# A three-layer sweep over an 8192 x 8192 matrix: part of the upper triangle by seven products in place of eight

## The chip, the cores and the metric

The kernel runs on one core of one Trainium2 chip. Times are device microseconds of that core from the start to the end of an execution. The trace is one profiled execution, taken by the hardware profiler: for each engine the instructions with start and duration, and the inferred releaser of every wait. TensorE (PE) does matrix products, with its weight loads (PEld) shown apart; VectorE (DVE), ScalarE (ACT) and GpSimd (POOL) work on tiles in SBUF; SyncE (SP) only issues DMA transfers. Each engine takes its instructions in order; they wait for each other by semaphores.

## What is computed

Four graph layers over the same adjacency matrix `adj`, 8192 x 8192 in float32, and node features `x`, 8192 x 64:

```python
def reference(x, adj, L0_gnn_u, L1_gnn_W, L1_gnn_b, L2_gnn_W, L3_gnn_W):
    h = relu(layernorm(x));  x = x + adj @ (h * (u >= 0.1) / 0.9)                            # layer 0
    h = relu(layernorm(x));  z = concat([h, (adj @ h + h) / deg]) @ W1 + b1                  # layer 1
    out = relu(z);           x = x + out / max(norm(out), 1e-12)
    h = relu(layernorm(x));  x = x + (dinv[:, None] * (adj + I) * dinv[None, :]) @ h @ W2    # layer 2
    h = relu(layernorm(x));  x = x + concat([h, adj @ h / (rowsum(adj) + 1)]) @ W3.T         # layer 3
    return x
```

Each layer needs `adj` times the states of the layer before it, row by row of the result, and row b's new states need all of row b.

## The kernel before, in words

`adj` is cut into 16 x 16 units of 512 x 512 (1 MB each, 128 partitions by 2048 numbers: four source tiles of 512 columns). Unit (b, g) holds what source block g gives to row b. A matmul has one source tile's states as weights (64 columns for one layer, 128 for two layers at once) and 512 columns of the unit as the moving operand; the result adds up in a PSUM bank of 128 x 512, whose lower 64 partitions (half 0) and upper 64 (half 1) are addressed apart. Each unit has four matmuls per layer; the trace shows each as two records.

The order is a sweep by phases, so that one loaded unit serves two layers where it can. Phase 1 goes down the rows for layer 0, with layer 1 in the part below the diagonal. Phase 2 goes up through the upper triangle for layer 1 (the units above the diagonal) and layer 2. Phase 3 goes down for layers 2 and 3, phase 4 does the rest of layer 3. `loads_in_order` writes out the load order for SP; the units go through a ring of 12 slots, a slot is reloaded when its unit has been let go (`unit_freed`), and diagonal units have two tiles of their own (`diag`).

The stretch that is changed is phase 2 after its head (rows 14 to 11 are the head, done by `head_first` and `head_second`): the loop over b from 10 down to 0 in the TensorE block. For each row b it takes the sources g from 15 down to b+1, 110 units in all, with `both_at_once` (line 563): four matmuls of 128 weight columns, layer 1's states (`h[1]`) in the lower half of the array and layer 2's (`h[0]`) in the upper, into one bank. Row b's source g needs the layer-2 states of row g, which the end of row g made (`await_unit` waits for them).

- After its first unit a row does `finish(1, b + 1)` (line 584): four matmuls of the gathered sums of the row before by the layer's weights, into Z. After its third it does `turn_own(1, b)` (line 627): two transposes of the row's own scaled states into HT, which ScalarE's `copy_hT` (line 398) copies to the upper half of y.
- VectorE does per row: `gather_1` (line 946: layer 1's sum from the bank to y), `end_layer_1` (lines 913 to 962, then the layer norm, lines 877 to 921: the new states of layer 2, with two square roots asked of ScalarE, `norm_root`, line 375), and `scale_own` (line 1031).
- ScalarE copies the layer-2 sum from the bank (`copy_part`, line 391) once Z is done.
- GpSimd makes constants at the start and clears one tile (line 355) in the head; in the loop it has nothing.

After the loop comes phase 3 with `head_first(3, ...)`, for which VectorE adds one to four diagonals (`add_one_again`, line 1006) after ScalarE has kept copies of them in `row_sum` (`keep_diag`). In phase 1 VectorE sums the units for the degrees (`sum_unit`, line 979, one unit-sized addition each).

## Time and profile before

| | |
|---|---|
| median of 3 runs | 1935.79 us (1935.2 to 1936.11) |
| span of the profiled execution | 1935.0 us |
| TensorE busy | 1892.8 us, 98% |
| VectorE busy | 855.0 us, 44% |
| ScalarE, GpSimd busy | 115.2 us, 3.3 us |
| DMA | 670.30 MB, 346 GB/s over the span |
| granted TensorE clock | 9 (nine tenths or more) in all 40 slices |

A page of the profile gives busy time by engine, the span in 40 slices, the chain of waits that ended last, and groups of instructions by line, operation and tile. The views used below are the page, the windows (busy time of each engine in a stretch), the timeline (instructions in order of time), the chain of waits in order of time, and the groups. Times on the chain and the timeline are us from the start of the span. Matmuls overlap in the records: one of 512 columns is recorded with about 0.59 us while the next starts 0.43 after it, so what counts is the step from one to the next.

### The profile page before, as it was taken

What the parts mean: (1) busy time and instruction counts of PE and PEld (TensorE: products, weight loads), DVE (VectorE), ACT (ScalarE), POOL (GpSimd) and SP (SyncE); (2) the same over time, 40 slices, a digit from 0 to 9 for tenths busy, and PEclk for the clock granted to TensorE, in tenths of its full rate; (3) what the DMA queues carried; (4) which work ended last, traced back from release to release, by engine and by line L of the source; (5) the groups of instructions that cost most, each with busy time, mean ns of one, the idle gap of its engine ahead of it and who ended that gap; (6) DMA issues with size and microseconds to landing.
All of it is one profiled execution on the core that took longest, in us unless ns stands there. A gap on an engine that the chain in (4) does not pass through costs nothing.

```text
span 1935.0 us, 17870 instructions
## 1 busy us (share of the span) xinstructions
PE 1892.8 (98%) x7216; PEld 740.1 (38%) x7216; DVE 855.0 (44%) x1023; ACT 115.2 (6%) x293; POOL 3.3 (0%) x18
## 2 busy tenths in 40 slices
PE   5899999999999999999999999999999999999998
PEld 1233333333333333444444444344444444344343
DVE  8677999998877763622112111321211110110322
ACT  0000000000000001100000000111100000000000
POOL 0000000000000000000000000000000000000000
PEclk9999999999999999999999999999999999999999
DMA  9999999999888885598888887497999989999998
GB/s 382 422 421 420 421 421 421 421 421 377 341 322 318 305 300 197 204 362 288 298 298 288 300 294 274 169 400 287 399 383 364 344 309 423 373 357 416 356 422 338
DMA packets 95168, 670.30 MB, mean 346 GB/s; under 512 B 11120, under 2 KB 13168, under 8 KB 14192
## 3 DMA queue, kind: packets, MB, share of 16 engines
q1 hardware_dynamic: 92160, 666.94, 87.9%
q10 hardware_dynamic: 2928, 2.23, 0.3%
q8 instruction: 59, 0.97, 0.2%
q14 instruction: 21, 0.17, 0.0%
HBM read 667.03 MB, written 2.10 MB: 346 GB/s over the span
## 4 chain that ended last, share of the span: by engine, by line
PE 86%; DVE 6%; DMA 6%; issue 1%; ACT 0%; SPq 0%; DVEq 0%
PE acc L534 45%; PE acc L563 36%; DMA ring<-stream_in 6%; PE Z L584 3%; DVE row_sum L979 1%; PE HT L627 1%; PE DEG L595 1%; DVE states L921 0%; DVE squares L880 0%; DVE centred L878 0%; PE DEG L604 0%; DVE inverse L881 0%; DVE mean L877 0%; DVE z_sb L913 0%; DVE x L962 0%
## 5 line engine op out<-in xcount | busy, mean ns | idle before, releaser
L534 PE MATMUL acc<-ring,states 128*64 128x512 f32 x4160 | 926.3, 596 | 34.2 <-DMA ring<-stream_in 26.5
L563 PE MATMUL acc<-ring,states 128*128 128x512 f32 x1792 | 778.8, 593 | 0.0
L534 PEld LDWEIGHTS acc<-ring,states 128*64 128x64 f32 x4160 | 296.6, 137 | 615.1 <-issue 586.2
L563 PEld LDWEIGHTS acc<-ring,states 128*128 128x128 f32 x1792 | 336.7, 190 | 414.5 <-issue 414.5
L979 DVE TENSOR_TENSOR row_sum<-row_sum,ring 128x2048 f32<-128x2048 f32 x187 | 428.5, 2292 | 9.1 <-DMA ring<-stream_in 3.9
L913 DVE TENSOR_TENSOR z_sb<-Z,deg_rsqrt 128x256 f32<-128x256 f32 x16 | 6.8, 425 | 336.8 <-PE Z L584 336.8
L946 DVE TENSOR_TENSOR y<-acc,y 64x512 f32<-64x512 f32 x16 | 11.1, 692 | 282.3 <-PE acc L563 274.9
L534 PE MATMUL acc<-diag,states 128*64 128x512 f32 x448 | 103.8, 595 | 1.1 <-DMA diag<-stream_in 1.1
L391 ACT COPY y<-acc 64x512 f32<-64x512 f32 x45 | 26.1, 580 | 1005.0 <-PE acc L534 730.6
L584 PEld LDWEIGHTS Z<-below,y 128*128 128x128 f32 x512 | 62.9, 191 | 50.6 <-issue 16.6
L1040 DVE TENSOR_TENSOR y<-acc,y 64x512 f32<-64x512 f32 x36 | 24.6, 683 | 111.3 <-PE acc L534 111.0
L584 PE MATMUL Z<-below,y 128*128 128x64 f32 x512 | 69.6, 279 | 2.2 <-DVE y L1041 2.2
L534 PEld LDWEIGHTS acc<-diag,states 128*64 128x64 f32 x448 | 32.5, 137 | 67.5 <-issue 64.7
L1006 DVE TENSOR_TENSOR diag<-diag,ident 128x384 f32<-128x384 f32 x12 | 6.7, 559 | 106.8 <-ACT row_sum L410 106.8
L979 DVE TENSOR_TENSOR row_sum<-ring 128x2048 f32<-128x2048 f32 x16 | 36.7, 2292 | 31.6 <-DMA ring<-stream_in 30.7
L929 DVE TENSOR_TENSOR x<-Z,x 128x256 f32<-128x256 f32 x16 | 6.8, 425 | 71.9 <-PE Z L584 71.6
L985 DVE TENSOR_TENSOR row_sum<-row_sum,diag 128x2048 f32<-128x2048 f32 x16 | 36.7, 2293 | 1.7 <-DMA diag<-stream_in 1.1
L375 ACT ACTIVATE rooted<-to_root 128x4 f32<-128x4 f32 (+1 forms) x68 | 14.0, 206 | 331.3 <-DVE to_root L867 303.2
L398 ACT COPY y<-HT 64x256 f32<-64x256 f32 x64 | 23.4, 365 | 153.9 <-PE HT L627 153.5
L877 DVE TENSOR_REDUCE mean<-x 128x4 f32<-128x256 f32 (+1 forms) x52 | 25.0, 481 | 7.7 <-DMA y<-u_in 6.0
L1041 DVE TENSOR_TENSOR y<-acc,y 64x512 f32<-64x512 f32 x36 | 24.9, 693 | 1.2
L913 DVE TENSOR_TENSOR z_sb<-Z,deg_clipped_inverse 128x256 f32<-128x256 f32 x16 | 6.8, 424 | 38.5 <-PE Z L584 38.4
(78 smaller groups left out, 363.2 us busy)
## 6 DMA issues: line engine op xcount, KB each, us to landing
ring<-stream_in SPq DMA_DIRECT2D x604, 1024.0 KB, 9.0
diag<-stream_in SPq DMA_DIRECT2D x28, 1024.0 KB, 11.5
x<-x_in SPq DMA_DIRECT2D x4, 512.0 KB, 6.9
y<-u_in SPq DMA_DIRECT2D x4, 512.0 KB, 8.7
x_out<-x ACTq DMA_DIRECT2D x16, 128.0 KB, 7.1
below<-w_in ACTq DMA_DIRECT2D x6, 16.0 KB, 5.8
bias<-b_in ACTq DMA_DIRECT2D x1, 32.0 KB, 9.8
```

The costliest lines, as they stand in the source:

```text
L391: nc.scalar.copy(own_y(b, 1 if layer == 2 else 0), half_of(bank, half)).then_inc(part_copied, 1)
L398: done = nc.scalar.copy(by_parity[:, parity], turned)
L534: return nc.tensor.matmul(half_of(bank, half), h[layer % 2][:, J], moving, start=start, stop=stop)
L563: done = nc.tensor.matmul(acc[bank][:, :], states[:, J * 2 * F:(J + 1) * 2 * F], source_tile(slot(key), k), start=first and k == 0, stop=l ...
L584: mm_z = nc.tensor.matmul(Z[:, t * F:(t + 1) * F], own_y(b)[:, t * P:(t + 1) * P], below[:, layer, :], start=True, stop=True)
L595: nc.tensor.matmul(DEG[k * QUARTER:(k + 1) * QUARTER, :], pick(key[1]), source_tile(slot(key), k), start=key == (1, 0, PE_SUMS[0][0]), sto ...
L627: mm_t = nc.tensor.transpose(HT[:, columns], scaled[n % 2][:, columns], ident[:, :])
L877: chain(nc.vector.tensor_reduce(m, by_tile(xs), X, ALU.add))
L979: nc.vector.tensor_tensor(row_sum[:, :], before, slot(key)[:, :], ALU.add).then_inc(unit_summed, 1 if count > 1 else 2)
L985: chain(nc.vector.tensor_tensor(row_sum[:, :], row_sum[:, :], diag_slot(1, b)[:, :], ALU.add))
L1040: chain(nc.vector.tensor_tensor(own_y(r, 0), half_of(bank, 0), own_y(r, 0), ALU.add))
L1041: nc.vector.tensor_tensor(own_y(r, 0), half_of(bank, 1), own_y(r, 0), ALU.add).then_inc(group_folded, 1)
```

## The change

Rows 10 to 1 of the loop are taken as five pairs (hi, lo), and sources above them as pairs (s1, s2). For such a group of four units (a **four**: A11 = (hi, s1), A12 = (hi, s2), A21 = (lo, s1), A22 = (lo, s2)) and the states B of the two sources in the two layers, the eight products of 2 x 2 blocks are replaced by seven (Strassen's scheme in Winograd's form). There are 2, 3, 4, 4 and 4 fours in the pairs, 17 in all.

- VectorE makes four new units per four from those in the ring, one unit-sized operation each: the sum A21 + A22 (into `row_sum` or `row_totals`) and A11 - A21 in `first_forms`, and the two that overwrite A11 and A12 in `last_forms`. The latter wait until TensorE has used the plain ones (`first_taken`, `second_taken`).
- GpSimd makes four combinations of states per source pair once (128 x 256 each), into the `diag` tiles, which are free until phase 3.
- TensorE does the products with weights of 64 columns, in slots of two products at a time, one in each half: an even four (`four_even`) in four slots, P2 with P1, P5 with P4, P7 with P6, and P3 with P1 of the next four ("P1 again", in a bank of its own); an odd four (`four_odd`) in three, P2 with P4, P5 with P6, P7 with P3. The products add up in banks over the fours of a pair (`GATHERS`).
- The unit (lo, hi) next to the diagonal is used for layer 1 in its own pair and loaded again for layer 2 ("again", "behind") in the next: `near_diagonal` does both as one slot, and in the first and the last pair one of the two is alone. The sources that make no pair are done by `plain_both`, one slot for each unit. The loads rise from 110 to 115 units.
- VectorE puts the sums together (`combine`, `combine_low`, `add_behind`) in place of `gather_1` and ScalarE's `copy_part`, with 64 x 512 additions.
- Row 0 is no longer the last row: two of its units stand at the start of every pair (`cover`) and the other five after the last.
- `finish` for both rows of a pair and the two transposes of the next pair stand between and behind these units; then TensorE waits for `pair_taken`. SP's diagonal loads of phase 3 wait for the last pair's end.

```diff
+PAIRS = [(10, 9), (8, 7), (6, 5), (4, 3), (2, 1)]
+SOURCE_PAIRS = [(15, 14), (13, 12), (11, 10), (9, 8)]
+FOURS = [[sp for sp in SOURCE_PAIRS if sp[1] > hi] for hi, lo in PAIRS]
+FOURS_BEFORE = [sum(len(fours) for fours in FOURS[:p]) for p in range(len(PAIRS) + 1)]
+PLAIN = [list(range(min(s for sp in FOURS[p] for s in sp) - 1, PAIRS[p][0], -1)) for p in range(len(PAIRS))]
+COVER = [[15, 14], [13, 12], [11, 10], [9, 8], [7, 6], [5, 4, 3, 2, 1]]
...
-BANK_UP = {13: 0, 12: 2, 11: 4, 14: 3, 10: 1}
-for b in range(9, -1, -1):
-    BANK_UP[b] = BANK_UP[b + 5]
+BANK_UP = {13: 0, 12: 2, 11: 4, 14: 3, 0: 1}
+GATHERS = {"P2": (0, 0), "P1": (0, 1), "P5": (2, 0), "P4": (2, 1), "P7": (4, 0), "P6": (4, 1),
+           "P1 again": (3, 0), "P3": (3, 1), "plain": (5, 0), "behind": (5, 0)}
...
-    for b in range(LAST - 1 - HEAD, -1, -1):
-        out += [(2, b, g) for g in range(LAST, b, -1)]
+    for p, (hi, lo) in enumerate(PAIRS):
+        out += [(2, 0, g) for g in COVER[p]]
+        for i, (s1, s2) in enumerate(FOURS[p]):
+            if i == len(FOURS[p]) - 1:
+                out += [("again", *PAIRS[p - 1][::-1])] if p else []
+                out += [(2, lo, hi)]
+            out += [(2, lo, s1), (2, lo, s2), (2, hi, s1), (2, hi, s2)]
+        out += [(2, b, g) for g in PLAIN[p] for b in (hi, lo)]
+    out += [(2, 0, g) for g in COVER[-1][:-1]] + [("again", *PAIRS[-1][::-1]), (2, 0, COVER[-1][-1])]
...
+            gp.wait_ge(*diag_let_go(1, LAST))
+            for n, (s1, s2) in enumerate(SOURCE_PAIRS):
+                gp.wait_ge(*state(2, s2))
+                if n > 0:
+                    gp.wait_ge(states_formed, n)
+                (b11, b12), (b21, b22) = [[of_row_states(layer, b) for layer in (1, 2)] for b in (s1, s2)]
+                t1, t2, t3, t4 = [formed((s1, s2), t) for t in (1, 2, 3, 4)]
+                nc.gpsimd.tensor_tensor(t1, b12, b11, ALU.subtract).then_inc(gp_step, 1)
+                nc.gpsimd.tensor_tensor(t3, b22, b12, ALU.subtract).then_inc(gp_step, 1)
+                gp.wait_ge(gp_step, 7 + 3 * n + 2)
+                nc.gpsimd.tensor_tensor(t2, b22, t1, ALU.subtract).then_inc(gp_step, 1)
+                gp.wait_ge(gp_step, 7 + 3 * n + 3)
+                nc.gpsimd.tensor_tensor(t4, b21, t2, ALU.subtract).then_inc(states_formed, 1)
...
+            for p in range(len(PAIRS)):
+                act.wait_ge(*pair_done(p))
+                if p > 0:
+                    act.wait_ge(pair_taken, 3 * p)
+                nc.scalar.copy(pair_sum(0), product("P1")).then_inc(p1_copied, 1)
+                for b in PAIRS[p + 1] if p < len(PAIRS) - 1 else [0]:
+                    copy_hT(1, b)
+                for b in PAIRS[p]:
                     norm_root()
                     norm_root()
-                copy_hT(1, b)
-                if b == 0:
-                    for r in ADDED[:HEAD]:
-                        keep_diag(r)
+            act.wait_ge(*fours_taken(FOURS_BEFORE[-1] - 1))
...
+            def four_even(p, i):
+                (hi, lo), (s1, s2) = PAIRS[p], FOURS[p][i]
+                n, last = FOURS_BEFORE[p] + i, i == len(FOURS[p]) - 1
+                a11, a12, a21, a22 = [(2, b, g) for b in (hi, lo) for g in (s1, s2)]
+                await_unit(a12, 1)
+                await_unit(a11, 1)
+                for k in range(TPR):
+                    two = nc.tensor.matmul(product("P2"), h[1][:, s2 * TPR + k], source_tile(slot(a12), k),
+                                           start=i == 0 and k == 0, stop=False)
+                    one = nc.tensor.matmul(product("P1"), h[1][:, s1 * TPR + k], source_tile(slot(a11), k),
+                                           start=i == 0 and k == 0, stop=i >= len(FOURS[p]) - 2 and k == TPR - 1)
+                two.then_inc(second_taken, 1)
+                one.then_inc(first_taken, 1)
+                pe.wait_ge(states_formed, SOURCE_PAIRS.index((s1, s2)) + 1)
+                pe.wait_ge(unit_formed, 4 * n + 1)
+                await_unit(a22, 2)
+                for k in range(TPR):
+                    five = nc.tensor.matmul(product("P5"), formed((s1, s2), 1)[:, k], source_tile(first_sum[n % 2], k),
+                                            start=i == 0 and k == 0, stop=last and k == TPR - 1)
+                    four = nc.tensor.matmul(product("P4"), formed((s1, s2), 4)[:, k], source_tile(slot(a22), k),
+                                            start=i == 0 and k == 0, stop=False)
+                five.then_inc(sum_taken, 1)
+                four.then_inc(unit_freed, 1)
+                pe.wait_ge(unit_formed, 4 * n + 3)
+                for k in range(TPR):
+                    seven = nc.tensor.matmul(product("P7"), formed((s1, s2), 3)[:, k], source_tile(slot(a21), k),
+                                             start=i == 0 and k == 0, stop=last and k == TPR - 1)
+                    nc.tensor.matmul(product("P6"), formed((s1, s2), 2)[:, k], source_tile(slot(a11), k),
+                                     start=i == 0 and k == 0, stop=last and k == TPR - 1)
+                seven.then_inc(unit_freed, 1)
+                pe.wait_ge(unit_formed, 4 * n + 4)
+                if not last:
+                    t1, t2 = FOURS[p][i + 1]
+                    await_unit((2, hi, t1), 1)
+                for k in range(TPR):
+                    if not last:
+                        one = nc.tensor.matmul(product("P1 again"), h[1][:, t1 * TPR + k],
+                                               source_tile(slot((2, hi, t1)), k), start=i == 0 and k == 0,
+                                               stop=i >= len(FOURS[p]) - 3 and k == TPR - 1)
+                    three = nc.tensor.matmul(product("P3"), h[0][:, s2 * TPR + k], source_tile(slot(a12), k),
+                                             start=i == 0 and k == 0, stop=False)
+                if not last:
+                    one.then_inc(first_taken, 1)
+                three.then_inc(unit_freed, 2)
+            def four_odd(p, i):
...
+                pe.wait_ge(states_formed, SOURCE_PAIRS.index((s1, s2)) + 1)
+                await_unit(a12, 1)
+                await_unit(a22, 2)
...
+                two.then_inc(second_taken, 1)
+                pe.wait_ge(unit_formed, 4 * n + 3)
...
+                five.then_inc(sum_taken, 1)
+                six.then_inc(unit_freed, 1)
+                pe.wait_ge(unit_formed, 4 * n + 4)
...
+                seven.then_inc(unit_freed, 1)
+                three.then_inc(unit_freed, 2)
...
+            def behind_last():
+                hi, lo = PAIRS[-1]
+                await_unit(("again", lo, hi), 2)
+                pe.wait_ge(pair_taken, 3 * len(PAIRS))
...
+            for p, (hi, lo) in enumerate(PAIRS):
+                cover(COVER[p][0])
+                if p > 0:
+                    finish(1, PAIRS[p - 1][0])
+                cover(COVER[p][1])
+                if p > 0:
+                    finish(1, PAIRS[p - 1][1])
+                turn_own(1, hi)
+                turn_own(1, lo)
+                if p == 0:
+                    pe.wait_ge(*gathered(1, 11))
+                    pe.wait_ge(part_copied, PARTS.index((2, 11)) + 1)
+                else:
+                    pe.wait_ge(pair_taken, 3 * p)
+                for i in range(len(FOURS[p])):
+                    if i == len(FOURS[p]) - 1:
+                        near_diagonal(p)
+                    if i % 2 == 0:
+                        four_even(p, i)
+                    else:
+                        four_odd(p, i)
+                for g in PLAIN[p]:
+                    plain_both(p, g)
+            cover(COVER[-1][0])
+            finish(1, PAIRS[-1][0])
+            cover(COVER[-1][1])
+            finish(1, PAIRS[-1][1])
+            turn_own(1, 0)
+            cover(COVER[-1][2])
+            cover(COVER[-1][3])
+            behind_last()
+            cover(COVER[-1][4])
...
+            def first_forms(p, i):
+                (hi, lo), (s1, s2) = PAIRS[p], FOURS[p][i]
+                n = FOURS_BEFORE[p] + i
+                a11, a21, a22 = (2, hi, s1), (2, lo, s1), (2, lo, s2)
+                dve.wait_ge(*loaded(a21))
+                dve.wait_ge(*loaded(a22))
+                if n >= 2:
+                    dve.wait_ge(*fours_taken(n - 2))
+                nc.vector.tensor_tensor(first_sum[n % 2][:, :], slot(a21)[:, :], slot(a22)[:, :],
+                                        ALU.add).then_inc(unit_formed, 1)
+                dve.wait_ge(unit_formed, 4 * n + 1)
+                dve.wait_ge(*loaded(a11))
+                nc.vector.tensor_tensor(slot(a21)[:, :], slot(a11)[:, :], slot(a21)[:, :],
+                                        ALU.subtract).then_inc(unit_formed, 1)
+                dve.wait_ge(unit_formed, 4 * n + 2)
+            def last_forms(p, i):
+                (hi, lo), (s1, s2) = PAIRS[p], FOURS[p][i]
+                n = FOURS_BEFORE[p] + i
+                a11, a12 = (2, hi, s1), (2, hi, s2)
+                dve.wait_ge(first_taken, n + 1)
+                nc.vector.tensor_tensor(slot(a11)[:, :], first_sum[n % 2][:, :], slot(a11)[:, :],
+                                        ALU.subtract).then_inc(unit_formed, 1)
+                dve.wait_ge(unit_formed, 4 * n + 3)
+                dve.wait_ge(second_taken, n + 1)
+                nc.vector.tensor_tensor(slot(a12)[:, :], slot(a12)[:, :], slot(a11)[:, :],
+                                        ALU.subtract).then_inc(unit_formed, 1)
+                dve.wait_ge(unit_formed, 4 * n + 4)
+            def combine(p):
+                hi, lo = PAIRS[p]
+                y_hi, y_lo, some, more = own_y(hi, 0), own_y(lo, 0), pair_sum(0), pair_sum(1)
+                dve.wait_ge(*pair_done(p))
+                chain(nc.vector.tensor_tensor(y_hi, product("P2"), y_hi, ALU.add))
+                dve.wait_ge(p1_copied, p + 1)
+                chain(nc.vector.tensor_tensor(some, product("P1 again"), some, ALU.add))
+                nc.vector.tensor_tensor(y_hi, some, y_hi, ALU.add).then_inc(sums_ready, 1)
+                dve.wait_ge(*gathered(1, hi))
+                chain(nc.vector.tensor_tensor(some, product("P6"), some, ALU.add))
+                chain(nc.vector.tensor_tensor(more, product("P7"), some, ALU.add))
+                chain(nc.vector.tensor_tensor(y_lo, more, y_lo, ALU.add))
+                nc.vector.tensor_tensor(y_lo, product("P4"), y_lo, ALU.add).then_inc(sums_ready, 1)
+                dve.wait_ge(*gathered(1, lo))
+                chain(nc.vector.tensor_tensor(pair_sum(0, 1), product("P5"), some, ALU.add))
+                nc.vector.tensor_tensor(pair_sum(1, 1), product("P5"), more, ALU.add).then_inc(pair_taken, 1)
+                dve.wait_ge(pair_taken, 3 * p + 1)
+                begin_layer_1(hi)
+                nc.vector.tensor_tensor(own_y(hi, 1), product("P3"), pair_sum(0, 1), ALU.add).then_inc(pair_taken, 1)
+                dve.wait_ge(pair_taken, 3 * p + 2)
+            def combine_low(p):
+                lo = PAIRS[p][1]
+                dve.wait_ge(z_done, rank(1, lo) + 1)
+                nc.vector.tensor_tensor(own_y(lo, 1), product("plain"), pair_sum(1, 1),
+                                        ALU.add).then_inc(pair_taken, 1)
+                dve.wait_ge(pair_taken, 3 * p + 3)
+            def add_behind(p):
+                hi, lo = PAIRS[p]
+                dve.wait_ge(*freed(("again", lo, hi)))
+                nc.vector.tensor_tensor(own_y(lo, 1), product("behind"), own_y(lo, 1),
+                                        ALU.add).then_inc(behind_added, 1)
+                dve.wait_ge(behind_added, p + 1)
...
+            for p, (hi, lo) in enumerate(PAIRS):
+                if p > 0:
+                    combine(p - 1)
+                first_forms(p, 0)
+                if p > 0:
+                    combine_low(p - 1)
+                last_forms(p, 0)
+                first_forms(p, 1)
+                last_forms(p, 1)
+                if p > 0:
+                    end_layer_1(PAIRS[p - 1][0], begun=True)
+                for i in range(2, len(FOURS[p])):
+                    first_forms(p, i)
+                    if i == len(FOURS[p]) - 1:
+                        add_behind(p - 1)
+                    last_forms(p, i)
+                if p > 0:
+                    end_layer_1(PAIRS[p - 1][1])
+                for b in PAIRS[p + 1] if p < len(PAIRS) - 1 else [0]:
+                    scale_own(1, b)
+            combine(len(PAIRS) - 1)
+            end_layer_1(PAIRS[-1][0], begun=True)
+            combine_low(len(PAIRS) - 1)
+            end_layer_1(PAIRS[-1][1])
+            add_behind(len(PAIRS) - 1)
+            gather_1(0)
```

`cover(g)` is `both_at_once` on unit (0, g). In `near_diagonal` (which waits for layer 2's states of the pair before it, `await_unit("again", 2)`), `plain_both` and `behind_last` each k does one matmul per half as above; `plain_both` waits for both layers' states of its source and, in the lower row's first unit, for `behind_added`.

## Rows read from the trace of the kernel before

**Rows 1.** The page: busy time, VectorE by slice, GB/s by slice, and the loop's matmuls.

```profile
PE 1892.8 (98%) x7216; PEld 740.1 (38%) x7216; DVE 855.0 (44%) x1023; ACT 115.2 (6%) x293; POOL 3.3 (0%) x18
...
DVE  8677999998877763622112111321211110110322
...
GB/s 382 422 421 420 421 421 421 421 421 377 341 322 318 305 300 197 204 362 288 298 298 288 300 294 274 169 400 287 399 383 364 344 309 423 373 357 416 356 422 338
...
L563 PE MATMUL acc<-ring,states 128*128 128x512 f32 x1792 | 778.8, 593 | 0.0
```

**Rows 2.** Windows: length, then busy PE, PEld, DVE, ACT, POOL; clock, DMA share, GB/s.

```profile
807.39:1200.06 392.67, 391.33 (x983) 177.13 (x982) 70.41 (x192) 21.74 (x63) 0.00 (x0) 1.00 0.86 308
440.00:640.00 200.00, 200.00 (x950) 68.20 (x948) 157.03 (x104) 7.20 (x15) 0.00 (x0) 1.00 0.89 337
```

**Rows 3.** Timeline at the loop's end: start, duration, engine, line, tiles, idle time before.

```profile
1200.26 0.69 DVE L946 TENSOR_TENSOR y<-acc,y 64x512 f32<-64x512 f32 x1 [41.73 <-PE acc L563]
```

**Rows 4.** Chain of waits in row 3 of the loop: start, duration, what.

```profile
1020.72 34.34 PE acc L563 x80
1055.05 0.85 PE Z L584 x8
```

**Rows 5.** The same chain, at half-width stretches of phases 1 and 3.

```profile
703.75 34.48 PE acc L534 x160
...
1226.91 7.02 PE acc L534 x32
...
1243.70 3.63 PE acc L563 x8
...
1257.85 5.29 PE acc L534 x16
...
1285.57 5.30 PE acc L534 x24
1290.87 1.03 PE Z L584 x8
```

**Rows 6.** Timeline, end of row 4 in the loop (rows between left out).

```profile
1008.99 0.69 DVE L946 TENSOR_TENSOR y<-acc,y 64x512 f32<-64x512 f32 x1 [28.00 <-PE acc L563]
1012.22 1.00 PE L584 MATMUL Z<-below,y 128*128 128x64 f32 x8
...
1013.26 0.42 DVE L913 TENSOR_TENSOR z_sb<-Z,deg_clipped_inverse 128x256 f32<-128x256 f32 x1 [3.58 <-PE Z L584]
1013.72 0.42 DVE L950 TENSOR_TENSOR z_sb<-z_sb,bias 128x256 f32<-128x256 f32 x1
...
1019.34 0.42 DVE L921 SCALAR_TENSOR_TENSOR states<-centred,inverse 128x256 f32<-128x256 f32 x1
...
1020.28 0.44 PE L627 MATMUL HT<-ident,scaled 128*128 128x128 f32 x2
...
1020.75 0.74 ACT L398 COPY y<-HT 64x256 f32<-64x256 f32 x2 [1.85 <-PE HT L627]
```

**Rows 7.** Groups by shape, whole span: busy us, mean ns of one, idle before.

```profile
L979 DVE TENSOR_TENSOR row_sum<-row_sum,ring 128x2048 f32<-128x2048 f32 x187 | 428.5, 2292 | 9.1 <-DMA ring<-stream_in 3.9
...
L979 DVE TENSOR_TENSOR row_sum<-ring 128x2048 f32<-128x2048 f32 x16 | 36.7, 2292 | 31.6 <-DMA ring<-stream_in 30.7
...
L946 DVE TENSOR_TENSOR y<-acc,y 64x512 f32<-64x512 f32 x16 | 11.1, 692 | 282.3 <-PE acc L563 274.9 <-ACT y L452 7.3
```

**Rows 8.** Timeline, phase 3: TensorE starts again after a wait for VectorE.

```profile
1223.25 0.42 DVE L921 SCALAR_TENSOR_TENSOR states<-centred,inverse 128x256 f32<-128x256 f32 x1
...
1223.82 2.06 PE L534 MATMUL acc<-ring,states 128*64 128x512 f32 x8 [1.17 <-DVE states L921]
```

**Rows 9.** The ring's loads in a stretch of the loop, issue to landing.

```profile
DMA to landing us min/median/max: 4.7/4.8/7.2
```

**Rows 10.** GpSimd's groups of instructions, whole span.

```profile
L337 POOL TENSOR_SCALAR_AFFINE_SELECT ident<-ident 128x128 f32<-128x128 f32 x1 | 0.3, 292 | 0.1
...
L355 POOL MEMSET y<- 64x512 f32 x1 | 0.5, 519 | 772.0 <-PE Z L584 772.0
```

149 lines of the change are left out of this document (121 added, 28 removed).

## Prediction

> **What bounds the kernel now.** I read the page first [rows 1]: TensorE is busy 98% of the span at full clock (the granted clock is 1.00 in every stretch I asked for), VectorE 44%, and in the slices of the upper-triangle loop (18 to 24 of 40) VectorE has one to two tenths. Then the windows [rows 2]: the loop, from its first matmul at 807.39 to 1200.06, where the last unit has issued (0.20 before VectorE reads it at 1200.26 [rows 3]), lasts 392.67 us; TensorE is busy 391.3 of them, VectorE 70.4, GpSimd 0, and the DMA moves 308 GB/s, where 421 to 423 are reached in other slices [rows 1]. The loop's matmuls (L563) have no idle time ahead of them at all [rows 1]. So in the one stage that the change touches the end is set by TensorE's column work: a change gains what it takes from TensorE, as long as VectorE, which gets new work, stays ahead.
>
> The chain of waits prices one unit [rows 4]: 10 whole units (128-wide weights, eight records each) take 34.34 us, so a **slot is 3.43 us**. A finish (Z) between whole units adds 0.85, a transpose pair 0.44 [rows 6]. 110 units make 377.4 us; finishes, transposes and their small waits are the other 15.3. Half-width matmuls run two at a time: 160 records, ten slots of 16, take 34.48 us, 32 take 7.02 with the switch to Z behind them [rows 5]. So a pair of half matmuls with different moving data costs the same slot. Between whole and half there is a surcharge: 3.63 for the last whole unit ahead of a transpose (0.20), 5.30 for one and a half slots ahead of Z (0.15), and 1.03 for a Z followed by halves (0.18) [rows 5]. A half without a partner costs its whole slot: a diagonal unit of row 4, which has none, and half a slot make 16 records in 5.29 us, where 24 records take 5.30 [rows 5].
>
> **The change on TensorE.** The 17 groups of four units are 68 units. By products they take 7 slots for two fours, 4 for an even one: 7+11+14+14+14 = 60 slots over the five pairs of rows. The five units next to the diagonal become six slots (one layer each, now paired across rows, the first and the last without a partner). The 11 sources left over stay at one slot per unit, 22; row 0 stays at 15. Sum 60+6+22+15 = 103 slots in place of 110: **7 x 3.43 = 24.0 us less**. That the two halves now carry different products into different banks costs nothing: the head steps (32 records in 7.02 [rows 5]) already do this. Against it: transposes come back to back, and the second waits until ScalarE has copied the first (0.74 for the copy [rows 6]), 1.75 for two in place of two times 0.44 and a small wait: over the loop +2.5. Whole-to-half switches, where no wait hides them: 5 x 0.15 at the pairs' ends and about 0.8 more: +1.6. TensorE alone would thus come out at -19.9, and VectorE decides what is left of it.
>
> **VectorE's prices.** A unit-sized operation (128x2048, two tiles of the ring) takes 2.292 us [rows 7], with the gap to the next 2.33. The 64x512 addition from PSUM takes 0.69, with its gap 0.73 [rows 7]; I take that for the additions in SBUF too. The scaled z is 0.46. The rest of the end of a row is 1013.72 to 1019.76 = 6.04 us, 6.5 with the z [rows 6]. A VectorE operation starts 0.20 us after the slot it waits for has issued (1012.22 less one slot is 1008.79, and it starts at 1008.99 [rows 6]); TensorE restarts 0.15 after the VectorE operation it waits for ends (1223.67 to 1223.82 [rows 8]). VectorE gets four unit-sized operations per four, 17 x 9.3 = 158 us, and 60 additions of 0.73 (eleven a pair and the one of the unit behind), 44, less ten gathers, 7; with the 70 it has that is some 265 of 398 us. So in total it fits; phase 1 shows TensorE undisturbed beside a VectorE that is busy 157 of 200 us [rows 2]. What matters is the order, since both engines take their work in order. I placed it on two time lines, E being the moment at which TensorE has issued a pair's last unit.
>
> (a) Entry of each pair after the first. TensorE: switch 0.15, cover 3.43, finish 0.86, cover 3.43, finish 0.86, two transposes 1.75: E+10.5. Then it waits for pair_taken, which combine_low raises. VectorE: E+0.20, ten additions and the z in combine (7.76), **both first_forms (4.66) which stand ahead of combine_low**, combine_low 0.73: E+13.35, so TensorE starts at 13.5. Wait **3.0, four times: 12.1**.
> (b) Two fours, T being their start: the even one (four slots) ends at T+13.7, the odd one (three) at T+24.0. VectorE starts last_forms 0.20 after the first slot, at 3.6, and has the two at 6.0 and 8.3; TensorE asks for them at 6.9 and 10.3. The next first_forms follow at 10.6 and 12.95, ahead of their use at 17.2. The odd last_forms wait for P1 (13.7) and P2 (17.15): 16.25 and 19.7, used at 17.2 and 20.6. No wait, with 0.7 to 2 us of margin.
> (c) Third four. end_layer_1 of the upper row stands ahead of its first_forms: VectorE is through at 19.7+6.04 = 25.7, then 28.05, 30.4, and 32.7 for the first of last_forms. TensorE needs the first sum at T+27.4 (gets it at 28.2) and the next form at 31.6 (gets it at 32.9). **0.8 + 1.2 = 2.0, in three pairs: 6.0.** In the pair (8, 7) the slot beside the diagonal comes first and needs row 10's new states: 25.9 against 24.0, 1.9, and hides the rest.
> (d) The plain source after the last four needs the states of the lower row before it: in (8, 7) 1.2, in (6, 5) 55.6+0.15 against 53.4 = 2.3. (The 55.6 is the fourth four's last form, at 49.1, and 6.5; the 53.4 is seven slots after the 28.2 of (c), with its 1.2.) In the last two pairs other sources come first: none.
> (e) Last pair's end: row 0's source 2 waits for row 2's states, for whose root ScalarE comes late, as it has the transpose of row 0 ahead of it: 2.0.
> Waits together 12.1+6.0+1.9+3.5+2.0 = **25.5 us**. Net: -24.0 + 2.5 + 1.6 + 25.5 = +5.6. With stretches added instead the loop is 398.1 against 392.7, **+5.5 us**: the first pair 43.1, then 64.6, 76.2 (as 13.5 of entry, 53.4 of fours, 2.3 of wait and 6.9 for one plain source), 87.6, 101.3, and 25.4 for the end of row 0. With gaps of 0.02 to 0.03 more per operation and 0.05 per wait it is +9; with the small ones all less, +3.4.
>
> Other edits at nothing: ScalarE's P1 copy is 0.58 beside VectorE's first addition; its ten copies of parts go; the five extra loads (115 units in 398 us, one per 3.46, while one lands in 2.5 us at 421 GB/s) lie inside the margin, and every four has its four units issued over 10 us before VectorE wants them, against 4.8 us median from issue to landing [rows 9]. SP's diagonal load that now waits for the last pair comes behind ring loads that are freed later anyhow. row_sum is kept for the diagonals only after the last four; ScalarE's four copies end before row 0's gather, as before. What follows the loop is as before and moves along.
>
> GpSimd's 16 subtractions (128x256) have no row of their kind; the nearest are 0.29 (128x128) and 0.52 (64x512 memset) [rows 10]. I take 0.3 to 0.8 each, the smaller and the sum of the two. The four in a row behind row 10's new states leave 3 us or more to spare. Whether they slow VectorE is not in the trace: nothing to, at worst, their whole time.
> The Trainium skill speaks against this part (GPSIMD Engine Reference, Specifications and Key points): GpSimd shares its SBUF interfaces with VectorE, with contention for instructions with two SBUF inputs, which all forms are; section 3.1 gives about 2.6 cycles per element at 1.2 GHz, an estimate of 0.6 to 0.7 us for one of these. No run here shows it yet.
>
> **Rivals.**
> Forecast, 65%: as placed, +5.5, from +3 to +9. About a third of it (+3.9 or less) would be within 0.2%.
> The entry is covered, 15%: faster. The mechanism is (a): if VectorE gets through its list at a pair's entry while TensorE is still in the two row-0 units, the four waits go; from 1.4 us less each the change is no loss, with all gone it is 5.5 - 12.1 = -6.6 us (1929), and with (c) to (e) gone too -19.9 (1916). For it: VectorE has over 130 us free in the loop, and some of its additions are from SBUF alone, for which I have no row. Against it: only two of the ten are, and the unit-sized operations, 4.66 of the 13.2 us, have 187 rows at 2.292.
> GpSimd holds VectorE up, 15%: the four operations follow directly on end_layer_1 of rows 10 and 8, just when VectorE does first_forms of the third four. If their 1.2 to 3.2 us are added to VectorE there, waits (c) and (d) grow by as much in two pairs, up to +4: 1943 to 1946. It decides from 1 us of hold-up per four operations. This is the Trainium skill's rule named above made into a time.
> Loads late, 5%: a four needs all its units at once. If the 7.2 us that is the longest landing [rows 9] became the rule at bursts of four, and each third four waited 2 us more for it, 6 us in all: 1947.
> That products don't save slots: excluded by [rows 5].
>
> **How the numbers follow.** The profiled execution has a span of 1935.0, the median of the runs is 1935.79, 0.8 above. 1935.0 + 5.5 + 0.8 = **1941.3 us**. For 8 in 10: down into the forecast's lower side and a little of the second case, 1934; up to GpSimd's case and a late load, 1948. A change under 0.2% (3.9 us) can hardly be told from none. Slower: 43 of the 65, and 15 and 5: 63%. Within: 22%. Faster 15%.
>
> **What would show it.** TensorE wait on y written by combine_low about 3 us, four times, and on ring units written by VectorE 0.8 and 1.2 us in the rows (6, 5), (4, 3), (2, 1); one wait each on states of rows 10, 9, 7 and 2. The loop some 398 us long, matmul busy time 20 us or more lower. It is wrong if these waits are absent (then the time is near 1916 to 1929), if half pairs with different products take over 3.5 us per slot, or if forms take clearly over 2.3 us.

## The result, and the profile after

| | before | after |
|---|---|---|
| median, lowest to highest | 1935.65 us (1935.20 to 1936.11, 4 runs) | 1951.56 us (1950.07 to 1953.65, 4 runs) |
| ratio, with 95% interval | | 1.0084 (1.0071 to 1.0098) |
| span of the profiled execution | 1935.0 us | 1951.0 us |
| TensorE busy | 1892.8 us | 1882.9 us |
| mean granted TensorE clock of the span | 1.00 | 0.993 |
| the loop, first matmul to its end | 392.8 us | 410.05 us |

The change makes the kernel 16 us slower. I had forecast 5.5 us slower, 1941.3, and a range up to 1948: the sign is right, the time lies outside the range. The page of after, with busy times and VectorE's and the clock's slices, answers to [rows 1]:

```profile
PE 1882.9 (97%) x7840; PEld 700.0 (36%) x7840; DVE 1047.9 (54%) x1141; ACT 112.0 (6%) x288; POOL 27.5 (1%) x34
...
DVE  8778999998888762857767564421211110110332
...
PEclk9999999999999999999999999999999999999999
```

TensorE works 9.9 us less, and the kernel is longer: the rest is standing still. VectorE has four to seven tenths in the slices of the loop, where it had one or two. The row of the clock shows nothing, since a slice is 49 us long; it takes short windows to see it, as below.

The loop alone, as a window (columns: length, busy time with count of TensorE, its weight loads, VectorE, ScalarE and GpSimd, granted clock, DMA share, GB/s), answers to [rows 2]:

```profile
806.95:1217.00 410.05, 382.05 (x1607) 138.63 (x1606) 262.00 (x310) 18.53 (x58) 17.89 (x8) 0.97 0.77 308
```

It is 17.3 us longer than before. The rest of the span gives 1.3 back (0.4 ahead of the loop, 0.9 behind), which makes the 16.0. The granted clock is 0.97, where it was 1.00. TensorE's waits in the loop (engine, line and what it waited for, then us in total, times, longest):

```profile
PE acc L783 <- DVE y L1251: 11.0, 4, 2.8
PE HT L718 <- ACT y L480: 4.6, 5, 0.9
PE acc L801 <- DVE ring L1217: 3.7, 3, 1.8
PE acc L877 <- DVE states L1167: 3.0, 2, 2.2
PE acc L651 <- DVE states L1167: 2.0, 1, 2.0
PE acc L793 <- issue: 1.8, 3, 0.6
PE DEG L861 <- DVE states L1167: 1.8, 1, 1.8
```

The first is (a), the wait for combine_low at the entries of four pairs. L801 and L793 are (c), L861 the slot beside the diagonal of (8, 7), L877 (d), L651 (e). HT behind ScalarE is the transposes. All of the forecast's waits are there: 23.3 us by this list, against its 25.5. (The list counts idle time from the end of a matmul's record, which lasts 0.59 us where the next would start after 0.43, so a wait behind a product costs some 0.2 more than it says.)

What the forecast did not have stands behind them. The timeline of the entry of (8, 7) (start, duration, engine, line, operation; in brackets the idle time and its releaser):

```profile
857.86 2.29 DVE L1203 TENSOR_TENSOR row_sum<-ring 128x2048 f32<-128x2048 f32 x1
...
858.75 0.39 PE L718 MATMUL HT<-ident,scaled 128*128 128x128 f32 x2
...
860.07 0.41 PE L718 MATMUL HT<-ident,scaled 128*128 128x128 f32 x2 [0.93 <-ACT y L480]
860.19 2.29 DVE L1207 TENSOR_TENSOR ring<-ring 128x2048 f32<-128x2048 f32 x1
...
862.51 0.68 DVE L1251 TENSOR_TENSOR y<-DEG,pair_sums 64x512 f32<-64x512 f32 x1
...
863.25 1.11 PE L783 MATMUL acc<-ring,states 128*64 128x512 f32 x1 [2.78 <-DVE y L1251]
...
864.16 1.06 PE L783 MATMUL acc<-ring,states 128*64 128x512 f32 x1
...
865.01 1.06 PE L783 MATMUL acc<-ring,states 128*64 128x512 f32 x1
...
868.17 0.59 PE L783 MATMUL acc<-ring,states 128*64 128x512 f32 x1
...
868.60 0.59 PE L783 MATMUL acc<-ring,states 128*64 128x512 f32 x1
```

Up to the restart at 863.25 everything is as placed: two first_forms, combine_low, a wait of 2.8. Then the matmuls start 0.85 us apart and take 1.06; from 868.17 they take 0.59 and start 0.43 apart. The same work at half the speed: TensorE runs at 1.2 GHz in place of 2.4 for about five us. The windows say the same (columns as above):

```profile
860.00:865.00 5.00, 2.16 (x6) 0.73 (x8) 3.13 (x3) 0.73 (x2) 0.00 (x0) 0.61 0.82 336
865.00:870.00 5.00, 5.00 (x20) 1.62 (x18) 0.65 (x1) 0.00 (x0) 0.00 (x0) 0.71 0.00 2
870.00:875.00 5.00, 5.00 (x26) 1.58 (x24) 4.93 (x3) 0.00 (x0) 0.00 (x0) 1.00 0.00 0
...
890.00:895.00 5.00, 3.44 (x16) 1.44 (x18) 4.56 (x7) 0.20 (x1) 3.51 (x2) 1.00 0.76 300
...
930.00:935.00 5.00, 4.74 (x12) 1.48 (x14) 0.21 (x1) 0.00 (x0) 0.00 (x0) 0.50 0.00 0
...
990.00:995.00 5.00, 5.00 (x16) 1.84 (x18) 0.57 (x2) 0.00 (x0) 0.00 (x0) 0.66 1.01 424
...
1205.00:1210.00 5.00, 5.00 (x9) 1.92 (x8) 4.35 (x13) 0.21 (x1) 0.00 (x0) 0.66 0.33 139
```

"Busy 5.00 of 5.00" beside 16 or 20 matmuls, where a window at full clock has 26: a busy TensorE is not one at its speed. Each slow stretch is measured as the length of the slot behind a wait (from its first matmul to the next slot's) less the same slot at full clock, in e2 below: the four entries +2.3, +2.9, +1.4 and +1.4, the plain source of (6, 5) at 990 +1.7, the end of row 0 at 1205 +1.7 (5.30 against 3.60). **Together 11.4 us**, the amount that the forecast lacks. In the loop's busy time it counts as work: it is 9.3 us lower than before's, where I had expected 20 or more, and with all at full clock, in e1 below, it is 20.8 lower. Not every wait has one: behind the 1.8 us at 891 the clock stays at 1.00, as the fourth row shows.

### The profile page after: what moved, and what is told of

It is laid out like the page before. It is cut to its first block, busy times and chain, and to the rows that moved or that the text cites. A ratio compares the mean times of both kernels' runs of the same rounds, so it can differ in the third digit from the quotient of the medians.

```text
span 1951.0 us, 19369 instructions
## 1 busy us (share of the span) xinstructions
PE 1882.9 (97%) x7840; PEld 700.0 (36%) x7840; DVE 1047.9 (54%) x1141; ACT 112.0 (6%) x288; POOL 27.5 (1%) x34
## 4 chain that ended last, share of the span: by engine, by line
PE 83%; DVE 10%; DMA 6%; issue 1%; ACT 0%; SPq 0%; DVEq 0%
PE acc L622 45%; PE acc L651 21%; DMA ring<-stream_in 6%; PE Z L675 2%; PE acc L877 2%; PE DEG L889 2%; PE acc L783 1%; PE acc L801 1%; PE acc L812 1%; DVE row_sum L1298 1%; PE acc L830 1%; PE acc L793 1%; DVE ring L1207 1%; DVE ring L1221 1%; DVE row_totals L1203 1%; PE DEG L861 1%
## 5 line engine op out<-in xcount | busy, mean ns | idle before, releaser
L622 PE MATMUL acc<-ring,states 128*64 128x512 f32 x4160 | 925.7, 596 | 33.7 <-DMA ring<-stream_in 25.9
L651 PE MATMUL acc<-ring,states 128*128 128x512 f32 x1032 | 453.4, 596 | 2.0 <-DVE states L1167 2.0
L651 PEld LDWEIGHTS acc<-ring,states 128*128 128x128 f32 x1032 | 193.5, 191 | 245.1 <-issue 245.1
L1359 DVE TENSOR_TENSOR y<-acc,y 64x512 f32<-64x512 f32 x36 | 24.6, 682 | 110.5 <-PE acc L622 110.3
L473 ACT COPY y<-acc 64x512 f32<-64x512 f32 x35 | 20.4, 582 | 736.5 <-PE acc L622 727.8
L783 PE MATMUL acc<-ring,states 128*64 128x512 f32 x72 | 40.6, 717 | 11.0 <-DVE y L1251 11.0
L1221 DVE TENSOR_TENSOR ring<-ring 128x2048 f32<-128x2048 f32 x17 | 39.4, 2316 | 9.9 <-PE acc L830 9.6
L877 PE MATMUL acc<-ring,states 128*64 128x512 f32 x88 | 41.3, 614 | 3.0 <-DVE states L1167 3.0
L1230 DVE TENSOR_TENSOR y<-acc,y 64x512 f32<-64x512 f32 x5 | 3.4, 683 | 75.8 <-PE DEG L889 75.8
L879 PE MATMUL acc<-ring,states 128*64 128x512 f32 x88 | 41.4, 614 | 0.0
L785 PE MATMUL acc<-ring,states 128*64 128x512 f32 x72 | 40.6, 717 | 0.0
```

Source lines behind the costliest of these rows:

```text
L473: nc.scalar.copy(own_y(b, 1 if layer == 2 else 0), half_of(bank, half)).then_inc(part_copied, 1)
L622: return nc.tensor.matmul(half_of(bank, half), h[layer % 2][:, J], moving, start=start, stop=stop)
L651: done = nc.tensor.matmul(acc[bank][:, :], states[:, J * 2 * F:(J + 1) * 2 * F], source_tile(slot(key), k), start=first and k == 0, stop=l ...
L783: two = nc.tensor.matmul(product("P2"), h[1][:, s2 * TPR + k], source_tile(slot(a12), k), start=i == 0 and k == 0, stop=False)
L785: one = nc.tensor.matmul(product("P1"), h[1][:, s1 * TPR + k], source_tile(slot(a11), k), start=i == 0 and k == 0, stop=i >= len(FOURS[p]) ...
L877: nc.tensor.matmul(product("P2"), h[1][:, J], source_tile(slot((2, hi, g)), k), start=False, stop=last and k == TPR - 1)
```

## Experiments

A kernel's distance is its ratio to the kernel before on the same chip, times 1935 us: after is at +16.3. Theory A: the waits are as forecast, and a half-clock stretch stands behind most of them, about 2 us each. Theory B: the slow steps come from something else in the changed program at those places, new moving data or a port shared with VectorE, and would stay without the wait. Theory C: the expected saving of 20 us of TensorE isn't there in full.

**e1_low_first: combine_low ahead of the first forms.**

```diff
                 if p > 0:
                     combine(p - 1)
-                first_forms(p, 0)
                 if p > 0:
                     combine_low(p - 1)
+                first_forms(p, 0)
                 last_forms(p, 0)
```

> One edit to the changed kernel: at a pair's entry VectorE does combine_low before the two unit-sized operations of first_forms, so that TensorE's wait for pair_taken (2.8 us, four times, 11.0 in all in the trace of the changed kernel) has no cause left: VectorE is through at E+9.6, TensorE asks at E+10.5. Theory A (a wait of about 3 us costs itself and then a stretch at half clock; the first slots after the four entries took 8.0 us over their normal length): 11 to 12 us and 8 us go, 19 to 20 in all, near 1932 us, and the granted clock is 1.00 at the entries. Theory B (the stretches at half clock come from something else in the new stretch, such as half-width products beside a busy VectorE): only the waits go, -11 to -12, near 1940 us, and the half-clock steps are still there.

Measured: 1931.91 us (1929.50 to 1933.51), ratio 0.9984 (0.9975 to 0.9992), so -3.1 us and 19.4 less than after. The entry waits are gone from the list; L801 (3.7), L877 (3.0), L651 (2.0), L861 (1.8) stand as they were. Moving two VectorE operations by one place takes away 11.0 us of waits and the 8.0 of half clock behind them (19.0). One line turns the change from a loss into a small gain.

The trace goes further than the medians. The loop of e1:

```profile
808.01:1195.43 387.42, 370.49 (x1607) 138.21 (x1607) 262.01 (x310) 18.54 (x58) 17.90 (x8) 1.00 0.81 326
```

It is 22.6 us shorter than in after, 11.0 of waits and the rest half clock, at (d) and (e) too: the waits of 2.2 and 2.0 us there are as long as in after, and the clock behind them is 1.00. So in after those two stretches are not the price of their waits alone.

**e2_filled: the entry wait stays, TensorE does unused work in it.** Three matmuls of states by states, whose result the next product overwrites, ahead of the wait:

```diff
                 else:
+                    for _ in range(3):
+                        nc.tensor.matmul(acc[0][:, :], states[:, 14 * TPR * 2 * F:(14 * TPR + 1) * 2 * F],
+                                         states[:, 15 * TPR * 2 * F:16 * TPR * 2 * F], start=True, stop=True)
                     pe.wait_ge(pair_taken, 3 * p)
```

> Work added to the changed kernel and none removed: while TensorE waits for pair_taken at the four entries it does three whole 512-column matmuls whose result is not used (six records, 2.57 us, into a bank that the next four starts anew). The wait for VectorE stays where it is. Theory A: the clock no longer falls at the four entries, 8 us less than the changed kernel, near 1943.5 us, with the loop's other two half-clock stretches unchanged. Theory B, and any in which the wait itself is the whole price: no change or up to 1 us more, 1951 to 1952.5.

Measured: 1942.08 us (1941.64 to 1944.72), ratio 1.0042 (1.0028 to 1.0056), +8.1 us: 8.2 less than after, though VectorE ends the waits no earlier in its list. The timeline and window of the same entry:

```profile
860.82 2.74 PE L990 MATMUL acc<-states 128*128 128x512 f32 x6
...
863.03 0.68 DVE L1254 TENSOR_TENSOR y<-DEG,pair_sums 64x512 f32<-64x512 f32 x1
...
863.76 0.64 PE L783 MATMUL acc<-ring,states 128*64 128x512 f32 x1 [0.21 <-DVE y L1254]
...
864.24 0.59 PE L783 MATMUL acc<-ring,states 128*64 128x512 f32 x1
```

```profile
860.00:865.00 5.00, 4.22 (x14) 1.72 (x16) 3.64 (x3) 1.15 (x4) 0.00 (x0) 1.00 0.88 362
```

The same product restarts at the same point of VectorE's list with 0.59 per matmul in place of 1.06. This rules theory B out for the entries, and by the medians it prices the clock there: 8.2 against the 8.0 read from the slots. One part of the expectation **fell**: the other two half-clock stretches were to stay, and in the profiled execution they are gone, with their waits of 2.2 and 2.0 us in place. The loop has the clock at 1.00 and is 11.3 us shorter than in after, not 8:

```profile
807.46:1206.17 398.71, 381.03 (x1632) 140.51 (x1631) 261.98 (x310) 18.53 (x58) 17.89 (x8) 1.00 0.79 317
```

So the match of 8.2 with 8.0 is in part luck.

**e3_long_wait and e4_short_wait: the waits alone, in the kernel before.** Rows 8, 6, 4 and 2 of the kernel before get a wait behind their finish on an operation in end_layer_1: in e3 the scaled z, in e4 an operation about 1.1 us ahead of it (the mean). No product, no new unit.

```diff
                         finish(1, b + 1)
+                        if b in STALLED:
+                            pe.wait_ge(marked, STALLED.index(b) + 1)
```

> The kernel before with nothing of the change: TensorE is made to wait at four places in the loop (rows 8, 6, 4, 2, behind the finish), until VectorE has scaled z_sb, about 3.2 us each by the trace of before. It measures the disputed price by itself. Theory A: 12.9 us of waits and 1.4 to 2.9 us each of half clock behind them, +18 to +24 us, 1954 to 1960. Theory B: +12.9, near 1948.7, clock 1.00 all through.

> The same four waits in the kernel before, ended earlier (VectorE's sum of squares), about 2.1 us each, 8.5 us in all. Theory A as I hold it (only the longer waits are followed by half clock; those of 1.3 to 2.0 us in the changed kernel mostly were not): +8.5 us, near 1944.3, clock 1.00. A rival form in which every wait costs in proportion: +12 to +14, near 1949.

Measured: e3 1954.91 us (1953.58 to 1956.98), ratio 1.0104 (1.0090 to 1.0118), +20.1. e4 1946.65 us (1946.04 to 1948.27), ratio 1.0063 (1.0050 to 1.0075), +12.2. Their waits, and a window around two of them each:

```profile
PE acc L565 <- DVE z_sb L971: 12.0, 4, 3.0
...
848.00:860.00 12.00, 9.00 (x23) 4.23 (x23) 5.94 (x17) 0.99 (x3) 0.00 (x0) 0.86 0.48 159
...
980.00:992.00 12.00, 9.00 (x21) 4.31 (x20) 5.94 (x17) 0.99 (x3) 0.00 (x0) 0.72 0.34 126
```

```profile
PE acc L565 <- DVE mean L965: 7.6, 4, 1.9
...
848.00:858.00 10.00, 8.11 (x26) 4.09 (x25) 5.94 (x17) 0.99 (x3) 0.00 (x0) 1.00 0.62 229
905.00:915.00 10.00, 8.11 (x22) 3.94 (x21) 5.94 (x17) 0.99 (x3) 0.00 (x0) 0.83 0.45 160
```

Four waits of 3.0 cost 20.1 us and not 12.0; the other 8.1 are the clock, in a kernel with no product and no new unit of the change, so theory B is out here too. A wait of 3 us thus costs 5. In e4 I had expected the waits to cost about their own length, with the clock left alone, and that **expectation fell**: 7.6 us of waits cost 12.2, which is what the rival form written there had (+12 to +14). In one of the four places the clock stays at 1.00, in the other three it falls (0.83), behind waits of the same 1.9 us. So 1.9 is not safe; it is the smaller chance of the same loss.

**e5_no_late_forms: what GpSimd costs VectorE.** e1 without GpSimd's subtractions for the two later source pairs; that part of the computation is left out.

```diff
                 t1, t2, t3, t4 = [formed((s1, s2), t) for t in (1, 2, 3, 4)]
+                if n >= 2:
+                    nc.gpsimd.memset(t4[:, 0, 0:1], 0.0).then_inc(states_formed, 1)
+                    continue
```

> The kernel of e1 without GpSimd's subtractions for the source pairs (11, 10) and (9, 8); their weights are left as they lie, so the products P4 to P7 of these fours are left out of the computation in effect. In the changed kernel these eight operations take up to 2.8 us each where VectorE does unit-sized additions beside them, against 0.7 to 0.9 where it does not, and two of VectorE's take 2.7 in place of 2.3. If the two engines hold each other up: TensorE's wait for GpSimd (0.7 us in the rows (8, 7)) and 0.8 us of the wait for the third four's form in (6, 5) go, -1.5 to -2 us against e1, near 1930. If the long operations are only GpSimd's own slowness, only the 0.7 goes: within 1 us of e1.

Measured: 1931.19 us (1928.93 to 1932.13), ratio 0.9978 (0.9969 to 0.9986), 1.2 less than e1; the two intervals overlap, so the time alone doesn't settle it. The lines do. In after, GpSimd takes 0.72 for one subtraction where VectorE does small operations, and 2.83 beside VectorE's forms; the form that runs when GpSimd starts keeps its 2.29, the next takes 2.70 (five forms in all do):

```profile
803.34 0.72 POOL L432 TENSOR_TENSOR diag<-states 128x256 f32<-128x256 f32 x1 [10.50 <-DVE states L1167]
...
959.08 2.29 DVE L1203 TENSOR_TENSOR row_totals<-ring 128x2048 f32<-128x2048 f32 x1
...
959.13 2.83 POOL L432 TENSOR_TENSOR diag<-states 128x256 f32<-128x256 f32 x1 [60.46 <-DVE states L1167]
...
961.41 2.70 DVE L1207 TENSOR_TENSOR ring<-ring 128x2048 f32<-128x2048 f32 x1
```

and without the subtractions, in e5, the same form is back at 2.29:

```profile
951.26 2.29 DVE L1210 TENSOR_TENSOR ring<-ring 128x2048 f32<-128x2048 f32 x1
```

The wait for the forms (L801) falls from 3.7 us to 2.9, all of it in (6, 5). The contention is real, and on the path it is worth 0.8 us here; TensorE's short wait for GpSimd in (8, 7) only moves, into L877's there (0.8 to 1.1). That both engines slow down agrees with the Trainium skill (GPSIMD Engine Reference, Key points: shared SBUF interfaces, contention with VectorE instructions of two SBUF inputs), which gives no size for it: here it is 0.4 us on a 2.29 us form, and nearly four times the time for GpSimd.

**e7_no_forms: TensorE's part alone.** After, with VectorE's four operations per four cut to one column, so the new units are left out:

```diff
-                nc.vector.tensor_tensor(slot(a21)[:, :], slot(a11)[:, :], slot(a21)[:, :],
+                nc.vector.tensor_tensor(slot(a21)[:, 0:1], slot(a11)[:, 0:1], slot(a21)[:, 0:1],
                                         ALU.subtract).then_inc(unit_formed, 1)
```

> The changed kernel with VectorE's four unit-sized operations per four cut to one column each (the new units are left out of the computation; all waits, copies and products stay). It measures what the change gives on TensorE alone. By the sum of the prediction: -24.0 of slots, +2.5 for the transposes, +1.6 for the switches, +2.0 for the last pair's end and up to 2 of half clock behind it: 16 to 18 us under the kernel before, ratio 0.991, near 1917 to 1919. If half-width products in different banks cost more than a slot, or if the saved slots are not there, it stays above 1925.

Measured: 1919.80 us (1919.15 to 1920.52), ratio 0.9921 (0.9908 to 0.9935), -15.3 us. Of the waits (a) to (e) only (e), 2.0, is left in the loop. The forecast was -17.9 (-19.9 and the 2.0 of (e)), and the loop in the trace is 17.6 shorter than before's 392.8:

```profile
808.45:1183.61 375.16, 368.47 (x1608) 135.62 (x1607) 115.55 (x310) 18.54 (x58) 5.74 (x8) 1.00 0.83 337
```

The whole time fell less; outside the loop, where they do the same work, profiled executions differ by up to 2.7 us (1542.2 us in before, 1539.6 in e3), so the loop is the better measure. TensorE's own part is -19.6, and theory C is out: the slots are saved; what VectorE's order makes TensorE wait, with the clock behind it, eats them.

**e9_wait_for_p3: the other way to free the entry.** combine_low stays behind the first forms; TensorE waits for one count less at the entry, and for combine_low's only in near_diagonal, the first place that needs the bank:

```diff
             def near_diagonal(p):
...
                 if p > 0:
+                    pe.wait_ge(pair_taken, 3 * p)
                     before_hi, before_lo = PAIRS[p - 1]
...
-                    pe.wait_ge(pair_taken, 3 * p)
+                    pe.wait_ge(pair_taken, 3 * p - 1)
```

> The changed kernel with one number changed in TensorE's wait at a pair's entry: it waits for P3 to have been read (pair_taken 3p-1) and no longer for combine_low (3p), which it needs only before the slot next to the diagonal starts its bank anew; VectorE's order stays. If the entry's 13 us are the price of that wait and not of VectorE's work as such: TensorE asks at E+10.5, P3 has been read at E+8.0, no wait and no half clock at the entries, the same time as e1, 1931 to 1933 us. If VectorE's order of e1 was what helped, the wait comes back at the second slot of the first four and it stays above 1936.

Measured: 1931.87 us (1931.03 to 1933.20), ratio 0.9983 (0.9974 to 0.9991), as e1, with no entry waits. The wait was for a bank that the products at the entry don't touch.

**e6_reordered and e8_unfilled: the rest of the waits, and a version that beats both.** The full computation, with each wait of the list taken up where it stands: the entry wait as in e9, row 0's unit 14 moved ahead of (6, 5)'s plain source, the transposes apart (one on either side of the second row-0 unit and its finish; in the first pair behind its first and its second slot), near_diagonal of (8, 7) behind a slot of its third four, end_layer_1 of the upper row in two halves around last_forms of the third four, the later states formed by VectorE. Two waits that are left are filled with four unused matmuls each. Its core:

```diff
                 for i in range(2, len(FOURS[p])):
                     first_forms(p, i)
+                    if p > 1 and i == 2:
+                        end_layer_1(PAIRS[p - 1][0], begun=True, half=0)
+                    last_forms(p, i)
+                    if p > 1 and i == 2:
+                        end_layer_1(PAIRS[p - 1][0], half=1)
...
-                    last_forms(p, i)
...
+                if p == 1:
+                    fill((1, lo))
```

e8 is e6 without the two fills.

> The whole computation, with the change's products and the order of the work made over: TensorE waits at a pair's entry only until P3 has been read (pair_taken 3p-1), the two transposes stand apart, row 0's source 14 is kept for the place ahead of (6, 5)'s plain source, end_layer_1 of the upper row is halved around last_forms of the third four, VectorE makes the state combinations of the two late source pairs itself, and two short waits are filled with unused matmuls. Theory A with the prediction's prices: against e1 -3.7 us for the transposes, -6.5 for the waits of the third fours, -2 to -4 for the plain sources and the slot beside the diagonal, -0.7 for GpSimd, and up to -2 of half clock: 1914 to 1919 us. If the waits merely move to the next place in VectorE's queue: 1925 or more.

> The kernel of e6 without its two groups of unused matmuls, so that the wait ahead of (8, 7)'s plain source and the one ahead of row 0's source 2 stand open again at about 2 us each. By theory A, as e4 has changed it (waits of about 2 us are followed by half clock at some places and not at others): 0 to 4 us more than e6, with times that differ from run to run by up to 2 us. If fillings only matter for waits near 3 us: as e6, within 0.5 us.

Measured: e6 **1918.18 us** (1917.64 to 1918.83), ratio 0.9912 (0.9899 to 0.9926), -17.0 us against before and 33 against after. e8 1920.02 us (1919.73 to 1920.72), ratio 0.9922 (0.9909 to 0.9936). The loop up to row 0's end in e6:

```profile
805.00:1185.00 380.00, 376.95 (x1641) 139.60 (x1639) 267.35 (x327) 19.12 (x59) 2.64 (x4) 1.00 0.84 337
```

TensorE idles 3 of 380 us at full clock, with VectorE as busy as in after (267.35 us): VectorE's amount of work was never the trouble, the order was, VectorE's and TensorE's. In e8 two waits come back (2.6 and 2.0 us), and only behind the longer one the clock falls:

```profile
PE acc L897 <- DVE states L1188: 2.6, 1, 2.6
...
PE acc L657 <- DVE states L1188: 2.0, 1, 2.0
```

```profile
900.00:905.00 5.00, 2.77 (x8) 1.04 (x10) 2.44 (x8) 0.20 (x1) 0.00 (x0) 0.69 1.01 419
```

The fills are worth 1.9 us, by medians, though they do no work: about what one half-clock stretch costs. The intervals of the two ratios overlap, so the time alone doesn't settle it; the window does.

## Why the prediction was right in sign and short in size

**The step that failed** is the sum of the waits, (a) to (e): each wait was priced at its own length, as if TensorE went on at full speed behind it. The runs put 11.4 us of half clock in the missing term, 8.0 of them at the entries (gone in e1 and e2) and 1.7 each at (d) and (e). I had read that the granted clock was 1.00 everywhere in the loop of before and took that for a property of the kernel. It was one of a loop in which the matmuls have no idle time ahead of them [rows 1]; adding waits takes that very condition away. I had even shown TensorE restarting after VectorE [rows 8], but after a wait too short to tell. The range's upper end, 1948, was built of further waits, all without the clock, so it was short as well: the span of 1951.0 less 11.4 would be 1939.6, beside the forecast's 1940.5 for it (1935.0 and 5.5). None of the three signs of error that I had named came (the waits are there, a slot at full clock stays at 3.43, the forms take 2.34 on the mean): the error was of a kind that I had not listed.

The loop's sum, forecast and measured, against the 17.3 us that it grew:

| term | forecast | measured |
|---|---|---|
| TensorE's own (slots, transposes, switches) | -19.9 | -19.6 (e7's loop, without its wait of 2.0) |
| waits (a) to (e) | 25.5 | 25.5 (what is left of the 17.3; 23.3 by the list) |
| half clock behind waits | none | 11.4 |

**TensorE.** The slots are saved (e7). The transposes cost what I took, 1.73 us for two in the timeline above (858.75 to 860.48) against 1.75. By the list of waits alone its own part would be -17.4, 2.5 us short. That hangs on the forms, since e7 is not short: e1's loop is 12.3 us longer than e7's, with 10.3 more of listed waits. The missing 2.0 stands at these nine waits and is for the most part what the list leaves out: across (e) in e7 two matmuls start 2.57 apart for an idle time of 1.98, where 0.43 is normal, 0.16 more than listed.

**VectorE's prices.** Right: forms 2.29 to 2.34 on the mean, additions 0.68, from SBUF alone too. These groups of after (the last columns are busy us, mean ns, idle us ahead) answer to [rows 7]; the 717 ns in the third is the half clock, seen from the groups, for these matmuls take 592 elsewhere:

```profile
L1207 DVE TENSOR_TENSOR ring<-ring 128x2048 f32<-128x2048 f32 x17 | 39.8, 2340 | 0.6
...
L1233 DVE TENSOR_TENSOR y<-degree_rows,y 64x512 f32<-64x512 f32 x5 | 3.4, 683 | 0.2
...
L783 PE MATMUL acc<-ring,states 128*64 128x512 f32 x72 | 40.6, 717 | 11.0 <-DVE y L1251 11.0
...
L812 PE MATMUL acc<-ring,states 128*64 128x512 f32 x64 | 28.8, 592 | 0.0
```

**(a)** Right: 2.8 us four times against 3.0, and its cause, the forms ahead of combine_low (e1). **(b)** Right: no wait there. **(c)** 5.5 by the list against 6.0, at the two places named, and 1.8 against 1.9 for (8, 7); but 0.8 of the 5.5 is GpSimd's (e5), which the forecast's case did not have, so that the closeness is in part luck. **(d)** 3.0 against 3.5. **(e)** 2.0 as forecast.

**The rivals.** "The entry is covered" did not happen by itself, but I had priced its gain at the waits alone, -12.1; e1 took 19.4. "GpSimd holds VectorE up" happened, with a subtraction at 2.83 us where I had bounded it by 0.8, but in about 1 us of the time and not 4. The four operations behind row 10's states did not have 3 us to spare: the last ends at 898.66, and TensorE waited for it until 898.72. Late loads: no wait for a DMA is in the loop's list.

**What stays open.** What decides whether a wait of about 2 us is followed by half clock. In after, 1.8 us at 891 was not and 2.2 us at 990 was; in e4 one of four equal waits was not; and the wait of 2.2 us for row 7's states (the one at 990) was followed by it in after, e5 and e9, and not in e1 and e2. Here are e9 and e1:

```profile
980.00:985.00 5.00, 5.00 (x16) 1.70 (x18) 0.64 (x2) 0.00 (x0) 0.00 (x0) 0.66 1.00 419
...
980.00:985.00 5.00, 4.89 (x24) 2.09 (x26) 0.76 (x2) 0.00 (x0) 0.00 (x0) 1.00 1.02 429
```

The wait of 2.0 us of (e) was followed by it in after alone, and not in the same wait of e1, e2, e5, e7, e8 and e9. The Trainium skill (TensorE: Matmul & The Clock Gate, HAM oscillation) describes waits that send the burst behind them back to half clock, for waits on DMAs; these runs show it for waits of 1.9 to 3.0 us on VectorE, in a stretch that is otherwise full.

## What to carry to other kernels

Where TensorE is busy throughout a stretch, price a new wait at its length and the slow restart that can stand behind it: here 3 us cost 5, and 1.9 us cost 3 on the mean, while some waits of 2.0 and 2.2 us cost no more than themselves. Before adding work to a helper engine with time to spare, write out its queue at the point where the critical engine next asks for something, and put what releases that engine first; the total load said "fits", and one place in the order was worth 19 us. Where a wait can't be moved, unused matmuls in it kept the clock up.

## What the runs showed of the hardware

- Behind waits of 2.8 to 3.0 us (all eight in after and e3) TensorE's fp32 matmuls of 512 columns ran at 1.2 GHz, in after for up to 6 us, in steps of 0.85 in place of 0.43, at a cost of 1.4 to 2.9 us each. Behind waits of 1.9 to 2.6 us it came at some and not at others: three of the four of 1.9 us in e4 had it, and one of seven of 2.0 us at the end of row 0. At (6, 5)'s plain source the fall came not at the restart but two steps later (matmul records of 0.61 and 0.64, then 1.06).
- A GpSimd subtraction of 128x256 fp32 takes 0.72 to 0.91 us with none of VectorE's unit-sized additions beside it, and 2.66 to 2.83 with one; of these additions, five in after took 2.70 us in place of 2.29.
